# Fetching x[dst] with fp32 products, and adding x on the vector engine, in a graph layer

## The chip, the cores and the metric

The kernel runs on one core of one Trainium2 chip. Its time is the device time of one execution in microseconds (us), as the median of several runs. One core has five engines with a queue of instructions each: TensorE (PE in the profile; its weight loads are listed apart as PEld), VectorE (DVE), ScalarE (ACT), GpSimd (POOL) and SyncE (SP, which only issues transfers here). An engine works through its queue in order; engines wait for each other by semaphores.

## The reference

```python
x_i = x[dst]                                    # x: 100000 x 48, 25000 edges
x_j = x[src]
tmp = jnp.concatenate([x_i, x_j, edge_attr], axis=1)      # 25000 x 128
h = jax.nn.relu(tmp @ W1 + b1)                  # 128 hidden
msg = h @ W2 + b2
out = jax.ops.segment_sum(msg, dst, num_segments=N_NODES)
x = _layernorm(x + out, axis=-1)                # over 48 columns
```

All is fp32, and `dst` is sorted.

## The kernel before

Since `dst` is sorted, the nodes are walked in blocks of 384 (128 partitions by J = 3 nodes), and the edges of a block lie one after another, at most 128 of them (for other inputs there is a general path, which does not run). Three blocks make a "super", called g in the code; there are 88 supers, the last two short. For each super the kernel does this:

- SP loads the edge rows (`load_edges`), the nodes' rows of x (`load_nodes`, into `xs`) and stores the result (`store`). POOL gathers x[src] row by row (`gather_xsrc`, three gathers per super) and does the last scaling of the norm (`scale`).
- DVE makes a one-hot matrix of each block, edges by 384 nodes (`make_onehot`). PE turns it (`turn_onehots`, `turn_last_onehot`, line 779), ACT copies it to SBUF (`onehot_t`, line 899).
- PE fetches x[dst] as a product of the turned one-hot with the rows of x (`fetch_xdst`, line 839). To be exact with bf16 products, DVE splits `xs` into three bf16 parts: the upper half of the fp32 word, the upper half of what is left (`x_rest`), and the rest of that (`x_low`). So there are 3 blocks x 3 node columns x 3 parts = 27 products of 48 columns.
- ACT places the result in `cat` (`place_xdst`, line 921), PE turns `cat` (`turn_cat`, line 773), ACT copies that (`copy_cat`, line 887), and PE forms the hidden layer (`hidden`, line 827; ACT's `relu`, line 915) and the messages (`messages`, lines 851 and 858).
- ACT copies the messages (`copy_msg`, line 894), DVE splits them in three (`less_high_msg`, line 1040, `less_middle_msg`, line 1047), and PE adds them to the nodes with 27 products with the one-hots (`sums`, line 819). x itself was put in the same PSUM bank ahead of that by three products of the parts of x with an identity (`add_nodes`, line 805), which stand between the products of the messages.
- The norm: DVE sums over the columns (`total_sum`, line 1024), subtracts the mean (`centre`, line 1033), ACT squares (`square`, line 926), DVE sums the squares (`total_squares`, line 1082), ACT takes the root (line 931), DVE inverts (line 1090), POOL scales (line 740).

What sets the order is `walk`: each engine has a list of (lag, stage), and step t of an engine runs each stage of its list, in the order written, for super t - lag. The first 16 steps are written out, then a loop of eight steps runs, then the rest is written out. Buffers have eight places (BODY) or two (SMALL). PE's list and ACT's, which the change leaves as they are:

```python
walk(pe, ((2, turn_cat), (0, turn_onehots), (5, sums), (2, hidden), (0, turn_last_onehot), (1, fetch_xdst),
          (3, messages)))
walk(act, ((7, root), (2, copy_cat), (4, copy_msg), (0, copy_onehots), (6, square), (0, copy_last_onehot), (2, relu),
           (1, place_xdst)))
```

So ACT's `square` of super t - 6 stands ahead of `place_xdst` of super t - 1, and PE's `turn_cat` of that super is the first stage of PE's next step.

Of the kernel before, what the change touches and what calls it, by code (L numbers as in the profile page):

```python
# [5 lines left out]
P = 128  # L6
# [4 lines left out]
ALU = mybir.AluOpType  # L11
# [363 lines left out]
def gnn_resnorm_kernel(nc, x, src, dst, edge_attr, W1, b1, W2, b2, out):  # L375
# [52 lines left out]
    with ExitStack() as ctx:  # L428
# [60 lines left out]
        onehot = sb("onehot", [P, BODY, SUPER, BLOCK], BF16)  # L489
        onehot_t = sb("onehot_t", [P, SMALL, SUPER, J * P], BF16)  # L490
        cat_t = sb("cat_t", [P, SMALL, SUPER * P])
# [4 lines left out]
        xs = sb("xs", [P, BODY, SD])  # L496
        x_rest = sb("x_rest", [P, BODY, SD])
        x_low = sb("x_low", [P, BODY, SD], BF16)
        ys = sb("ys", [P, BODY, SD])
# [50 lines left out]
        msg_split = sem("msg_split")  # L550
        x_rest_ready = sem("x_rest_ready")
        x_split = sem("x_split")
        dst_counted = sem("dst_counted")
# [97 lines left out]
        def _(sp):  # L651
# [41 lines left out]
            def load_nodes(g, r, v):  # L693
                if after(g, BODY):
                    sp.wait_ge(sum_done, g - BODY + 1)
                sp.dma_start(sbuf_rows(xs, g, v), dram_rows(x, g)).then_inc(x_in[v], 16)
# [53 lines left out]
        def _(pe):  # L750
# [47 lines left out]

            def add_nodes(g, v, i):

                n, blocks, jj = shape_of(g)
                part = (upper_half(flat_of(xs, g, v)), upper_half(flat_of(x_rest, g, v)), flat_of(x_low, g, v))[i]
                if i == 0 and after(g, SMALL):
                    pe.wait_ge(centred, g - SMALL + 1)
                pe.matmul(sum_ps[v % SMALL][0:n, 0:blocks * jj * D], ident_b[0:n, 0:n], part, start=(i == 0), stop=False)  # L805

            def sums(g, r, v):

                n, blocks, jj = shape_of(g)
                ps, t, m = sum_ps[v % SMALL], v % SMALL, slice(0, blocks * D)  # L810
                msg_parts = upper_half(msg[:, t, m]), upper_half(msg_rest[:, t, m]), msg_low[:, t, m]
                pe.wait_ge(msg_split, g + 1)
                if isinstance(g, int) and g == NS - 1:
                    for i in range(PARTS):
                        add_nodes(g, v, i)
                for k in range(blocks):
                    for j in range(jj):
                        for i, part in enumerate(msg_parts):
                            last = pe.matmul(ps[0:n, (k * jj + j) * D:(k * jj + j + 1) * D], onehot[:, v, k, j * n:(j + 1) * n],  # L819
                                             part[:, k * D:(k + 1) * D], start=False,  # L820
                                             stop=(k == blocks - 1 and j == jj - 1 and i == PARTS - 1))
                last.then_inc(sum_done, 1)
# [7 lines left out]
            def fetch_xdst(g, r, v):  # L830

                n, blocks, jj = shape_of(g)
                parts = upper_half(flat_of(xs, g, v)), upper_half(flat_of(x_rest, g, v)), flat_of(x_low, g, v)
                pe.wait_ge(x_split, g + 1)
                pe.wait_ge(onehot_t_ready, first_block(g) + blocks)
                for k in range(blocks):
                    for j in range(jj):
                        for i, part in enumerate(parts):
                            last = pe.matmul(xdst_ps[:, k * D:(k + 1) * D], onehot_t[0:n, v % SMALL, k, j * P:(j + 1) * P],  # L839
                                             part[:, (k * jj + j) * D:(k * jj + j + 1) * D],  # L840
                                             start=(j == 0 and i == 0), stop=(j == jj - 1 and i == PARTS - 1))
                last.then_inc(xdst_done, 1)

            def messages(g, r, v):
                n, blocks, jj = shape_of(g)
                pe.wait_ge(hid_t_ready, g + 1)
                if after(g, 1):
                    pe.wait_ge(msg_ready, g)


                pe.matmul(msg_ps[:, 0:blocks * D], ones_b[:, :], b2_parts[:, 0:blocks, :].rearrange("p b d -> p (b d)"),  # L851
                          start=True, stop=False)
                for k in range(SUPER):
                    if after(g, 1):
                        add_nodes(g - 1, (v - 1) % BODY, k)
                    if k >= blocks:
                        continue
                    last = pe.matmul(msg_ps[:, k * D:(k + 1) * D], hid_t[:, v % SMALL, k * P:(k + 1) * P], w2[:, :],  # L858
                                     start=False, stop=(k == blocks - 1))
                    if k == blocks - 1:  # L860
                        last.then_inc(msg_done, 1)

# [79 lines left out]
        def _(dve):  # L942
# [74 lines left out]
            def sums_of(g, t):  # L1017
                n, blocks, jj = shape_of(g)
                return sum_ps[t][0:n, 0:blocks * jj * D].rearrange("p (m d) -> p m d", d=D)

            def total_sum(g, r, v):
                n, blocks, jj = shape_of(g)
                dve.wait_ge(sum_done, g + 1)
                dve.tensor_reduce(total[0:n, v % SMALL, 0:blocks * jj], sums_of(g, v % SMALL), AX_X, ALU.add).then_inc(totalled, 1)  # L1024

            def centre(g, r, v):

                n, blocks, jj = shape_of(g)
                t, m = v % SMALL, blocks * jj
                dve.wait_ge(totalled, g + 1)  # L1030
                if after(g, BODY):
                    dve.wait_ge(y_out[v], 16 * r)
                dve.scalar_tensor_tensor(out=by_node(ys, g, v), in0=total[0:n, t, 0:m].unsqueeze(2).broadcast_to([n, m, D]),
                                         scalar=-1.0 / D, in1=sums_of(g, t), op0=ALU.mult, op1=ALU.add).then_inc(centred, 1)

# [31 lines left out]

            def less_high_x(g, r, v):
                dve.wait_ge(x_in[v], 16 * (r + 1))
                dve.tensor_tensor(flat_of(x_rest, g, v), flat_of(xs, g, v), upper_half(flat_of(xs, g, v)),  # L1070
                                  ALU.subtract).then_inc(x_rest_ready, 1)

            def less_middle_x(g, r, v):
                dve.wait_ge(x_rest_ready, g + 1)
                dve.tensor_tensor(flat_of(x_low, g, v), flat_of(x_rest, g, v), upper_half(flat_of(x_rest, g, v)),
                                  ALU.subtract).then_inc(x_split, 1)

            def total_squares(g, r, v):
# [5 lines left out]
            def invert(g, r, v):  # L1084
# [3 lines left out]
                if after(g, SMALL):  # L1088
                    dve.wait_ge(normed, g - SMALL + 1)
                dve.reciprocal(rstd[0:n, t, 0:m], std[0:n, t, 0:m]).then_inc(rstd_ready, 1)  # L1090

            walk(dve, ((6, total_sum), (-1, place_dst), (-1, less_high_x), (6, centre), (-1, less_middle_x),
                       (4, less_high_msg), (-1, make_onehot), (7, invert), (4, less_middle_msg), (6, total_squares)))
            dve.wait_ge(general_done, 1)
# [26 lines left out]
```

## Time and profile before

| | us |
|---|---|
| median of 3 timed runs | 494.03 |
| lowest, highest | 492.64, 494.47 |
| span of the profiled execution | 593.7 |
| PE busy | 430.8 |
| DVE busy | 383.0 |
| POOL busy | 351.2 |
| ACT busy | 292.1 |

The profiled execution is 99.7 us longer than the median of the timed runs. The rows that the text rests on are all from that execution. A row of the timeline gives the start from the beginning of the span and how long the instruction took from its start to its end; since an engine begins the next instruction ahead of the end of the last, what an instruction costs its engine is read from start to start. "x3" means that three instructions were merged in a row. In brackets stands how long the engine was idle before it and what ended that.

### The profile page before, as it was taken

To read this page: it belongs to the slowest core of one execution; us is meant where nothing else is said; L and a number is where in the kernel's file an instruction comes from. 1 tells how busy PE (TensorE), PEld (TensorE's weight loads), DVE (VectorE), ACT (ScalarE), POOL (GpSimd) and SP (SyncE) were. 2 spreads that over 40 slices of the span, in tenths; PEclk is the share of its full clock that TensorE was granted. 3 is DMA by queue.
4 is the path that set the end of the run, shared out by engine and by line. 5 is a ranking of instruction groups with operands and counts; after the bars stand their busy time and mean duration, and the time that the engine had idled before them with its cause. 6 is when DMAs were issued, how large, how long until landed. Compare 5 with 4: busy or idle time off the path is not lost.

```text
span 593.7 us, 19546 instructions
## 1 busy us (share of the span) xinstructions
PE 430.8 (73%) x6796; PEld 368.5 (62%) x6796; DVE 383.0 (65%) x1105; ACT 292.1 (49%) x795; POOL 351.2 (59%) x365
## 2 busy tenths in 40 slices
PE   1013378797888878788788878787888878887891
PEld 1012367676767767676667767675776767766690
DVE  5423148676766678676667666776667756877673
ACT  2212147464555556464555545464555545554662
POOL 2056616767665666666665666666666666757522
PEclk9999999988988899898989888989889989999996
DMA  7833313444433434344444344343443434444422
GB/s 181 286 64 67 68 25 82 86 110 87 110 84 81 108 84 108 83 108 82 100 89 94 94 83 108 81 109 82 88 100 83 108 83 107 86 108 85 105 64 73
DMA packets 118243, 56.92 MB, mean 96 GB/s; under 512 B 46019, under 2 KB 117185, under 8 KB 118205
## 3 DMA queue, kind: packets, MB, share of 16 engines
q1 hardware_dynamic: 109440, 48.35, 32.2%
q0 software_dynamic: 8448, 6.50, 8.6%
q10 hardware_dynamic: 318, 1.61, 1.0%
q8 instruction: 20, 0.33, 0.2%
q14 instruction: 17, 0.14, 0.1%
HBM read 33.80 MB, written 22.61 MB: 95 GB/s over the span
## 4 chain that ended last, share of the span: by engine, by line
PE 66%; issue 18%; another core or an unknown queue 6%; ACT 4%; DVE 3%; DMA 1%; ACTq 0%; POOL 0%; SPq 0%; POOLq 0%; DVEq 0%
PE bank L839 14%; PE bank L827 11%; PE bank L819 10%; PE bank L779 8%; PE bank L805 8%; PE bank L858 7%; PE bank L773 7%; ACT onehot_t L899 2%; DMA next_dst_i<-in_dst_dram 1%; PE bank L851 1%; ACT sq L926 1%; ACT hid_t L915 1%; ACT cat L921 0%; ACT msg L894 0%
## 5 line engine op out<-in xcount | busy, mean ns | idle before, releaser
L732 POOL DMA_INDIRECT cat<-in_x_dram,cat x264 | 267.9, 1015 | 201.1 <-DMA cat<-edge_table 135.7
L899 ACT ACTIVATE onehot_t<-bank 128x384 bf16<-128x384 bf16 (+1 forms) x261 | 119.3, 498 | 182.1 <-remote 129.4
L1024 DVE TENSOR_REDUCE total<-bank 128x9 f32<-128x432 f32 (+1 forms) x88 | 52.8, 599 | 87.6 <-remote 86.5
L839 PE MATMUL bank<-x_low,onehot_t 128*128 128x48 bf16 (+1 forms) x782 | 86.0, 185 | 27.4 <-issue 26.9
L839 PE MATMUL bank<-x_rest,onehot_t 128*128 128x48 bf16 (+1 forms) x782 | 85.8, 186 | 26.7 <-issue 26.6
L858 PEld LDWEIGHTS bank<-w,hid_t 128*128 128x128 f32 x522 | 101.5, 208 | 4.0 <-issue 2.8
L779 PEld LDWEIGHTS bank<-ident_b,onehot 128*128 128x128 bf16 (+1 forms) x782 | 65.2, 107 | 61.4 <-issue 48.1
L839 PE MATMUL bank<-xs,onehot_t 128*128 128x48 bf16 (+1 forms) x782 | 86.6, 186 | 22.5 <-issue 22.1
L779 PE MATMUL bank<-ident_b,onehot 128*128 128x128 bf16 (+1 forms) x782 | 80.6, 236 | 24.9 <-issue 24.9
L740 POOL TENSOR_TENSOR ys<-ys,rstd 128x432 f32<-128x432 f32 (+1 forms) x88 | 80.3, 912 | 23.6 <-DVE rstd L1090 20.5
L858 PE MATMUL bank<-w,hid_t 128*128 128x48 f32 x522 | 89.9, 255 | 2.5 <-issue 2.5
L839 PEld LDWEIGHTS bank<-x_low,onehot_t 128*128 128x128 bf16 (+1 forms) x782 | 65.4, 97 | 34.5 <-issue 33.9
L839 PEld LDWEIGHTS bank<-x_rest,onehot_t 128*128 128x128 bf16 (+1 forms) x782 | 65.8, 97 | 32.5 <-issue 31.9
L827 PE MATMUL bank<-cat_t,w 128*128 128x384 f32 (+1 forms) x176 | 83.6, 559 | 1.0 <-issue 0.7
L839 PEld LDWEIGHTS bank<-xs,onehot_t 128*128 128x128 bf16 (+1 forms) x782 | 67.2, 97 | 26.3 <-issue 25.7
L1040 DVE TENSOR_TENSOR msg_rest<-msg 128x144 f32<-128x144 f32 (+1 forms) x88 | 27.1, 308 | 75.4 <-issue 37.6
L887 ACT ACTIVATE cat_t<-bank 128x384 f32<-128x384 f32 (+1 forms) x88 | 42.9, 487 | 64.1 <-PE bank L773 54.8
L819 PE MATMUL bank<-msg,onehot 128*128 128x48 bf16 (+1 forms) x782 | 73.7, 188 | 0.5 <-issue 0.5
L1064 DVE TENSOR_SCALAR onehot<-node_of,dst_in_block 128x384 bf16<-128x384 f16 x260 | 73.8, 338 | 0.1
L819 PE MATMUL bank<-msg_rest,onehot 128*128 128x48 bf16 (+1 forms) x782 | 73.0, 187 | 0.4 <-issue 0.4
L819 PE MATMUL bank<-msg_low,onehot 128*128 128x48 bf16 (+1 forms) x782 | 72.9, 187 | 0.0
L773 PE MATMUL bank<-ident,cat 128*128 128x128 f32 x261 | 52.6, 316 | 25.9 <-ACT cat L921 18.9
(91 smaller groups left out, 910.8 us busy)
## 6 DMA issues: line engine op xcount, KB each, us to landing
xs<-in_x_dram SPq DMA_DIRECT2D x86, 216.0 KB
out_dram<-ys SPq DMA_DIRECT2D x86, 216.0 KB
cat<-edge_table SPq DMA_DIRECT2D x264, 17.0 KB
cat<-in_x_dram,cat POOLq DMA_INDIRECT x264
edge_table<-table_pm SPq DMA_DIRECT2D x4, 833.0 KB, 7.5
edge_pm<-in_edge_attr_dram ACTq DMA_DIRECT2D x2, 686.0 KB, 6.0
edge_pm<-in_edge_attr_dram SPq DMA_DIRECT2D x2, 686.0 KB, 6.0
edge_pm<-in_edge_attr_dram ACTq DMA_DIRECT2D x2, 91.9 KB, 7.3
```

What stands on the lines that cost most here:

```text
L732: pool.indirect_dma_start(cat[:, v, k, D:2 * D], None, x[:, :], bass.IndirectOffsetOnAxis(ap=cat[:, v, k, P + 1:P + 2].bitcast(I32), axis= ...
L740: pool.tensor_tensor(y, y, rstd[0:n, v % SMALL, 0:blocks * jj].unsqueeze(2).broadcast_to([n, blocks * jj, D]), ALU.mult).then_inc(normed, 1)
L773: last = pe.transpose(cat_ps[:, k * P:(k + 1) * P], cat[:, v, k, 0:P], ident[:, :])
L779: last = pe.transpose(onehot_ps[k % 2][0:n, j * P:(j + 1) * P], onehot[:, v, k, j * n:(j + 1) * n], ident_b[:, :])
L805: pe.matmul(sum_ps[v % SMALL][0:n, 0:blocks * jj * D], ident_b[0:n, 0:n], part, start=(i == 0), stop=False)
L819: last = pe.matmul(ps[0:n, (k * jj + j) * D:(k * jj + j + 1) * D], onehot[:, v, k, j * n:(j + 1) * n], part[:, k * D:(k + 1) * D], start=F ...
L827: pe.matmul(hid_ps[:, 0:blocks * P], w1[:, :], cat_t[:, v % SMALL, 0:blocks * P], start=True, stop=True).then_inc(hid_done, 1)
L839: last = pe.matmul(xdst_ps[:, k * D:(k + 1) * D], onehot_t[0:n, v % SMALL, k, j * P:(j + 1) * P], part[:, (k * jj + j) * D:(k * jj + j + 1 ...
L858: last = pe.matmul(msg_ps[:, k * D:(k + 1) * D], hid_t[:, v % SMALL, k * P:(k + 1) * P], w2[:, :], start=False, stop=(k == blocks - 1))
L899: act.activation(onehot_t[0:n, v % SMALL, k, 0:jj * P], onehot_ps[k % 2][0:n, 0:jj * P], ACT.Copy).then_inc(onehot_t_ready, 1)
L1024: dve.tensor_reduce(total[0:n, v % SMALL, 0:blocks * jj], sums_of(g, v % SMALL), AX_X, ALU.add).then_inc(totalled, 1)
L1064: last = dve.tensor_scalar(onehot[:, v, k, 0:n * jj], nodes[:, 0:n * jj], dst_in_block[:, v % SMALL, k:k + 1], None, ALU.is_equal)
```

## The change

x[dst] is fetched with the fp32 rows `xs` and an fp32 `onehot_t` by nine products instead of 27; the split of x and its two buffers go. The three identity products go too; DVE adds `xs` to the sums in PSUM and writes `ys` (`add_nodes`), and `total_sum` and `centre` work on `ys` in SBUF. DVE's list is in a new order. `load_nodes` and `sums` wait for the addition.

```diff
-        onehot_t = sb("onehot_t", [P, SMALL, SUPER, J * P], BF16)
+        onehot_t = sb("onehot_t", [P, SMALL, SUPER, J * P])
...
             def load_nodes(g, r, v):
                 if after(g, BODY):
-                    sp.wait_ge(sum_done, g - BODY + 1)
+                    sp.wait_ge(added, g - BODY + 1)
...
-            def add_nodes(g, v, i):
-
-                n, blocks, jj = shape_of(g)
-                part = (upper_half(flat_of(xs, g, v)), upper_half(flat_of(x_rest, g, v)), flat_of(x_low, g, v))[i]
-                if i == 0 and after(g, SMALL):
-                    pe.wait_ge(centred, g - SMALL + 1)
-                pe.matmul(sum_ps[v % SMALL][0:n, 0:blocks * jj * D], ident_b[0:n, 0:n], part, start=(i == 0), stop=False)
...
             def sums(g, r, v):
...
-                if isinstance(g, int) and g == NS - 1:
-                    for i in range(PARTS):
-                        add_nodes(g, v, i)
+                if after(g, SMALL):
+                    pe.wait_ge(added, g - SMALL + 1)
...
-                                             part[:, k * D:(k + 1) * D], start=False,
-                                             stop=(k == blocks - 1 and j == jj - 1 and i == PARTS - 1))
+                                             part[:, k * D:(k + 1) * D], start=(i == 0), stop=(i == PARTS - 1))
...
             def fetch_xdst(g, r, v):
...
-                parts = upper_half(flat_of(xs, g, v)), upper_half(flat_of(x_rest, g, v)), flat_of(x_low, g, v)
-                pe.wait_ge(x_split, g + 1)
+                rows = flat_of(xs, g, v)
+                pe.wait_ge(x_in[v], 16 * (r + 1))
...
-                        for i, part in enumerate(parts):
-                            last = pe.matmul(xdst_ps[:, k * D:(k + 1) * D], onehot_t[0:n, v % SMALL, k, j * P:(j + 1) * P],
-                                             part[:, (k * jj + j) * D:(k * jj + j + 1) * D],
-                                             start=(j == 0 and i == 0), stop=(j == jj - 1 and i == PARTS - 1))
+                        last = pe.matmul(xdst_ps[:, k * D:(k + 1) * D], onehot_t[0:n, v % SMALL, k, j * P:(j + 1) * P],
+                                         rows[:, (k * jj + j) * D:(k * jj + j + 1) * D],
+                                         start=(j == 0), stop=(j == jj - 1))
...
+            def add_nodes(g, r, v):
+                n, blocks, jj = shape_of(g)
+                dve.wait_ge(sum_done, g + 1)
+                if after(g, BODY):
+                    dve.wait_ge(y_out[v], 16 * r)
+                dve.tensor_tensor(by_node(ys, g, v), by_node(xs, g, v), sums_of(g, v % SMALL), ALU.add).then_inc(added, 1)
...
-            walk(dve, ((6, total_sum), (-1, place_dst), (-1, less_high_x), (6, centre), (-1, less_middle_x),
-                       (4, less_high_msg), (-1, make_onehot), (7, invert), (4, less_middle_msg), (6, total_squares)))
+            walk(dve, ((6, add_nodes), (-1, place_dst), (4, less_high_msg), (6, total_sum), (-1, make_onehot), (4, less_middle_msg),
+                       (6, centre), (7, invert), (6, total_squares)))
```

One step of DVE in the steady part of the program before. `msg` and `msg_rest` are the messages, `xs` the rows of x, `bank` the PSUM bank with the sums, `ys` the result:

```order
L1024 TENSOR_REDUCE total<-bank 128x9
L1054 TENSOR_TENSOR dst_in_block<-cat,block_start 128x3
L1070 TENSOR_TENSOR x_rest<-xs 128x432
L1033 SCALAR_TENSOR_TENSOR ys<-total,bank 128x432
L1075 TENSOR_TENSOR x_low<-x_rest 128x432
L1040 TENSOR_TENSOR msg_rest<-msg 128x144
L1064 TENSOR_SCALAR onehot<-node_of,dst_in_block 128x384 x3
L1090 RECIPROCAL rstd<-std 128x9
L1047 TENSOR_TENSOR msg_low<-msg_rest 128x144
L1082 TENSOR_REDUCE sq_total<-sq 128x9
```

The same step of DVE in the changed program:

```order
L1007 TENSOR_TENSOR ys<-xs,bank 128x432
L1041 TENSOR_TENSOR dst_in_block<-cat,block_start 128x3
L1027 TENSOR_TENSOR msg_rest<-msg 128x144
L1012 TENSOR_REDUCE total<-ys 128x9
L1051 TENSOR_SCALAR onehot<-node_of,dst_in_block 128x384 x3
L1034 TENSOR_TENSOR msg_low<-msg_rest 128x144
L1020 SCALAR_TENSOR_TENSOR ys<-total,ys 128x432
L1067 RECIPROCAL rstd<-std 128x9
L1059 TENSOR_REDUCE sq_total<-sq 128x9
```

`centre` (ys from total) stood ahead of the subtraction for `msg_rest`; it now stands behind it, behind the one-hots and behind `msg_low`, and one short instruction ahead of the sum of the squares.

PE at the end of a step before, from the last product of the fetch to the transposes that begin the next step (`w` is W2, `hid_t` the hidden layer):

```order
L839 MATMUL bank<-x_low,onehot_t 128x48
L851 MATMUL bank<-b_parts,ones_b 128x144
L805 MATMUL bank<-xs,ident_b 128x432
L858 MATMUL bank<-w,hid_t 128x48
L805 MATMUL bank<-x_rest,ident_b 128x432
L858 MATMUL bank<-w,hid_t 128x48
L805 MATMUL bank<-x_low,ident_b 128x432
L858 MATMUL bank<-w,hid_t 128x48
L773 MATMUL bank<-ident,cat 128x128 x3
```

And in the changed program, from the last transposes of the one-hots on:

```order
L776 MATMUL bank<-ident_b,onehot 128x128 x3
L825 MATMUL bank<-xs,onehot_t 128x48 x9
L837 MATMUL bank<-b_parts,ones_b 128x144
L840 MATMUL bank<-w,hid_t 128x48 x3
L770 MATMUL bank<-ident,cat 128x128 x3
```

The fetch is nine products in a row, and nothing stands between the products of the messages.

## Rows read from the trace of the kernel before

**Rows 1.** The page, busy us, share of the span and instructions of each engine:
```profile
PE 430.8 (73%) x6796; PEld 368.5 (62%) x6796; DVE 383.0 (65%) x1105; ACT 292.1 (49%) x795; POOL 351.2 (59%) x365
```

**Rows 2.** The waits: engine and line, waited for; us in total, times, longest:
```profile
PE bank L839 <- issue: 75.7, 161, 1.2
```

**Rows 3.** Busy time by stretch: stretch, length, each engine, granted clock, DMA share, GB/s:
```profile
83.47:569.50 486.03, 397.69 (x6396) 342.03 (x6395) 341.05 (x975) 265.12 (x736) 312.07 (x314) 0.93 0.42 93
```

**Rows 4.** Timeline of PE, an early step and a late one: start, us, instruction:
```profile
83.47 0.51 PE L773 MATMUL bank<-ident,cat 128*128 128x128 f32 x3
...
85.73 0.19 PE L839 MATMUL bank<-xs,onehot_t 128*128 128x48 bf16 x1
...
86.42 0.22 PE L851 MATMUL bank<-b_parts,ones_b 128*128 128x144 bf16 x1
...
86.67 0.32 PE L858 MATMUL bank<-w,hid_t 128*128 128x48 f32 x2
86.82 0.35 PE L805 MATMUL bank<-x_rest,ident_b 128*128 128x432 bf16 x1
...
87.50 0.51 PE L773 MATMUL bank<-ident,cat 128*128 128x128 f32 x3
...
569.50 0.51 PE L773 MATMUL bank<-ident,cat 128*128 128x128 f32 x3
```

**Rows 5.** Timeline of POOL, the gathers and the scaling:
```profile
92.08 0.95 POOL L732 DMA_INDIRECT cat<-in_x_dram,cat  x1 [0.30 <-issue]
93.33 0.95 POOL L732 DMA_INDIRECT cat<-in_x_dram,cat  x1 [0.30 <-issue]
94.79 0.91 POOL L740 TENSOR_TENSOR ys<-ys,rstd 128x432 f32<-128x432 f32 x1 [0.51 <-issue]
95.85 0.99 POOL L732 DMA_INDIRECT cat<-in_x_dram,cat  x1
```

**Rows 6.** Timeline of PE and of its weight loads, first steps (two windows):
```profile
65.64 0.90 PE L773 MATMUL bank<-ident,cat 128*128 128x128 f32 x3 [9.37 <-ACT cat L921]
...
70.00 0.73 PEld L858 LDWEIGHTS bank<-w,hid_t 128*128 128x128 f32 x3
...
70.00 1.37 PEld L858 LDWEIGHTS bank<-w,hid_t 128*128 128x128 f32 x6
```

**Rows 7.** Timeline of ACT, three places:
```profile
65.29 0.29 ACT L921 ACTIVATE cat<-bank 128x144 f32<-128x144 f32 x1 [9.11 <-remote]
...
84.02 0.49 ACT L887 ACTIVATE cat_t<-bank 128x384 f32<-128x384 f32 x1 [1.14 <-PE bank L773]
84.41 0.28 ACT L894 ACTIVATE msg<-bank 128x144 f32<-128x144 f32 x1
...
85.93 0.49 ACT L899 ACTIVATE onehot_t<-bank 128x384 bf16<-128x384 bf16 x1 [0.47 <-PE bank L779]
86.32 0.57 ACT L915 ACTIVATE hid_t<-bank,b1c 128x384 f32<-128x384 f32 x1
86.78 0.29 ACT L921 ACTIVATE cat<-bank 128x144 f32<-128x144 f32 x1
...
578.76 0.56 ACT L926 ACTIVATE sq<-ys 128x432 f32<-128x432 f32 x1 [0.71 <-DVE ys L1033]
```

**Rows 8.** Timeline of DVE, an early step and one at the end:
```profile
84.72 0.31 DVE L1040 TENSOR_TENSOR msg_rest<-msg 128x144 f32<-128x144 f32 x1 [2.40 <-ACT msg L894]
84.95 0.77 DVE L1064 TENSOR_SCALAR onehot<-node_of,dst_in_block 128x384 bf16<-128x384 f16 x3
85.64 0.30 DVE L1047 TENSOR_TENSOR msg_low<-msg_rest 128x144 bf16<-128x144 f32 x1
85.86 0.60 DVE L1024 TENSOR_REDUCE total<-bank 128x9 f32<-128x432 f32 x1
86.38 0.15 DVE L1054 TENSOR_TENSOR dst_in_block<-cat,block_start 128x3 f32<-128x3 f32 x1
...
578.12 0.60 DVE L1033 SCALAR_TENSOR_TENSOR ys<-total,bank 128x432 f32<-128x432 f32 x1
```

More of the change, by code:

```diff
@@ L550, in gnn_resnorm_kernel @@
         msg_split = sem("msg_split")
-        x_rest_ready = sem("x_rest_ready")
-        x_split = sem("x_split")
+        added = sem("added")
         dst_counted = sem("dst_counted")
@@ L852, in messages @@
                           start=True, stop=False)
[L853 to L857, printed above, removed]
+                for k in range(blocks):
                     last = pe.matmul(msg_ps[:, k * D:(k + 1) * D], hid_t[:, v % SMALL, k * P:(k + 1) * P], w2[:, :],
                                      start=False, stop=(k == blocks - 1))
-                    if k == blocks - 1:
-                        last.then_inc(msg_done, 1)
+                last.then_inc(msg_done, 1)
             walk(pe, ((2, turn_cat), (0, turn_onehots), (5, sums), (2, hidden), (0, turn_last_onehot), (1, fetch_xdst),
@@ L1019, in sums_of @@
                 return sum_ps[t][0:n, 0:blocks * jj * D].rearrange("p (m d) -> p m d", d=D)
+            def add_nodes(g, r, v):
[4 more added lines that the diff above has]
+                dve.tensor_tensor(by_node(ys, g, v), by_node(xs, g, v), sums_of(g, v % SMALL), ALU.add).then_inc(added, 1)
             def total_sum(g, r, v):
                 n, blocks, jj = shape_of(g)
-                dve.wait_ge(sum_done, g + 1)
-                dve.tensor_reduce(total[0:n, v % SMALL, 0:blocks * jj], sums_of(g, v % SMALL), AX_X, ALU.add).then_inc(totalled, 1)
+                dve.wait_ge(added, g + 1)
+                dve.tensor_reduce(total[0:n, v % SMALL, 0:blocks * jj], by_node(ys, g, v), AX_X, ALU.add).then_inc(totalled, 1)
             def centre(g, r, v):
@@ L1030, in centre @@
                 dve.wait_ge(totalled, g + 1)
[L1031 to L1034, printed above, removed]
+                y = by_node(ys, g, v)
+                dve.scalar_tensor_tensor(out=y, in0=total[0:n, t, 0:m].unsqueeze(2).broadcast_to([n, m, D]),
+                                         scalar=-1.0 / D, in1=y, op0=ALU.mult, op1=ALU.add).then_inc(centred, 1)
             def less_high_msg(g, r, v):
@@ L1066, in make_onehot @@
                 last.then_inc(onehot_ready, 1)
[L1068 to L1076, printed above, removed]
             def total_squares(g, r, v):
```

2 lines of the change are left out of this document (removed).

## The prediction

> **What bounds the kernel now.** I read the views in the order of the row groups. First the shares: no engine is above three quarters of the span, and PE, DVE and POOL are close to each other [rows 1], so what matters is the length of one step of each engine's loop, not the busy share. Then the waits: the largest of PE's are gaps ahead of the products of line 839 in which it waits for nothing that is shown, 75.7 us [rows 2]. Over the long middle stretch the granted clock is 0.93 on average [rows 3], that is, about 14% of the time at the lower of TensorE's two levels (1.2 GHz) and the rest at 2.4 GHz.
>
> An early step shows PE without any gap: transposes of `cat` start at 83.47 and again at 87.50 [rows 4], so PE's own work for one step (three blocks, one "super") takes **4.03 us** at the upper level. The same transposes start at 569.50 for g = 85, and 83.47 was g = 3: 82 steps in 486.0 us, 5.93 us each in the profiled run. POOL has its own minimum: gathers start 1.25 us apart (92.08, 93.33), one takes 0.95, and from the scaling to the next gather 1.06 passes (94.79, 95.85) [rows 5]: 1.25 + 1.25 + 0.95 + 1.06 = **4.51 us**.
>
> The profiled span is 593.7 us, the median of the timed runs 494.0, so profiling itself costs about 100 us. I take the 107.7 us outside the 82 steps (593.7 - 486.0) as the same in both; then a timed step is (494.0 - 107.7) / 82 = **4.71 us**. That fits POOL's 4.51 with small losses better than PE's 4.03, so the timed kernel seems to be held by POOL's queue, with PE about 0.7 us per step behind it. This split is an inference; the sum below uses only differences to 4.71.
>
> **The change on PE.** The fetch of x[dst] is 27 bf16 products in 0.69 us (85.73 to 86.42) [rows 4]. It becomes nine fp32 products. The nearest rows are the fp32 products of line 858, also 48 columns wide against 128x128 fp32 weights. Each leaves two records. In the first step, with no other product between them, three weight loads take 0.73 us and six take 1.37 [rows 6]: 0.213 us per record. That was at the lower level, for the three transposes beside them take 0.90 [rows 6] where they take 0.51 at the upper [rows 4]. Half of it is 0.107. The bounds: not below 0.075 (in the messages an fp32 product starts at 86.67 and the next identity product at 86.82 [rows 4], 0.15 us for two records, of which one has its load beside the product ahead), not above 0.213. I take 0.107 since only those rows have consecutive fp32 products: 18 records are 1.92 us, **+1.23** (bounds +0.66 and +3.1). The fp32 weights stay 128 wide, and the moving side is read as loaded, so there is nothing else.
>
> The three identity products per step go. The messages are then one bias product, 0.06, and six records: 0.70 in place of 1.08 (86.42 to 87.50 [rows 4]), **-0.38**. The 27 products of the sums stay; only their start and stop marks change. PE's own step: 4.03 + 1.23 - 0.38 = **4.88 us**.
>
> The Trainium skill, "FP8 and Floating Point Precision", section "TensorE Precision Notes", says that true FP32 takes four passes through the array. As an estimate from that, a product of 48 columns would be four times the 0.026 us of a bf16 one, 0.10 us; fetch 0.92, messages 0.37, PE's step 3.55. The trace disagrees, with 0.213 us per product at the upper level: it is the loads of weights that stand 0.213 us apart at the lower one [rows 6].
>
> **The change on DVE and ACT.** DVE loses two subtractions per step (0.52 us from start to start, like the reduction from 85.86 to 86.38 [rows 8]) and gains one addition of the same 432 columns, which I price the same; between 0.5 and 0.6. It is 0.5 us lighter. ACT writes `onehot_t` in fp32: the 384-column copy to fp32 has 0.49 us and the one to bf16 0.49 [rows 7], so nothing. SP's load of x now waits for the addition instead of the last product of the sums, half a step later; queued behind it are a store and the edge loads of two steps ahead, seven PE steps from their use, so I cost it at zero. The sums wait for the addition of two supers back, which stands one DVE step earlier; zero too. ys is written by the addition, an op earlier than by `centre`, with the store of eight supers back long done.
>
> What counts is the new order on DVE. Before, `centre`(g-6) stood ahead of the subtraction `less_high_msg`(g-4), so ACT's square had its input early. Now it stands behind `less_high_msg`, which waits for ACT's copy of the messages in the same step, and behind the total, the three one-hots and `less_middle_msg`. ACT's queue is strict: square waits for `centre`, and behind it stand the last one-hot copy, the relu and `place_xdst`, for which PE's next transposes wait. This closes a loop through all three engines within one step. From start to start, in us:
>
> PE's transposes to ACT's copy of cat 0.55 (83.47, 84.02); to the copy of msg 0.39 (84.41); to DVE's msg_rest 0.31 (84.72); to the next on DVE 0.23 (84.95); the total 0.52 (85.86 to 86.38); three one-hots 0.69 (84.95 to 85.64); msg_low 0.22 (to 85.86); `centre` to square 0.64 (578.12, 578.76); square to the next on ACT 0.46 (as relu, 86.32 to 86.78, of nearly the same length); the last one-hot copy 0.39 (85.93 to 86.32); relu 0.46; `place_xdst` to PE's transposes 0.35 (65.29, 65.64) [rows 4, 6 to 8].
>
> The sum is 0.55 + 0.39 + 0.31 + 0.23 + 0.52 + 0.69 + 0.22 + 0.64 + 0.46 + 0.39 + 0.46 + 0.35 = **5.21 us**. It is longer than PE's 4.88 and POOL's 4.51, and no queue can run ahead in it, as every member waits for one of the same step. PE's end of the fetch (transposes, sums, hidden layer, then 1.92 us: about 4.4 us after the step's start) comes before ACT reaches `place_xdst` at 4.86, so the fetch's own price hardly matters.
>
> **The forecast.** A step of 5.21 us holds at the upper clock. Where the clock is at 1.2 GHz, PE's 4.88 becomes 9.76 and holds the step. With 14% of the time there, the mean is 1 / (0.86/5.21 + 0.14/9.76) = 5.57. Without the slack of 0.7 us that PE has today nothing absorbs such stretches, but the timed run may have fewer of them; I take the middle, 5.39. Then 494.0 + 82 x (5.39 - 4.71) = 550, and some 2 us for the first fetch at the lower clock (18 x 0.213 = 3.8 against twice 0.69): **552 us**. Its own range goes from 5.21 (494 + 41 + 2 = 537) to 5.57 (567).
>
> **Rivals.** (1) The loop has slack that I don't see, and PE alone decides: 82 x (4.88 - 4.71) = +14, with the first fetch 510 us. For it: all handoffs are single rows. Against: the waits in the code leave no second route. (2) The clock. PE now waits 0.3 us in every step, its work in between has changed, and the trace shows that the granted clock is not held at the upper level throughout [rows 3]; if the lower level held 30% of the time, the step were 6.06 and the time 605. Against: 5.93 us per step in the profile left PE waiting more than that, and the clock was at the lower level only 14% of the time. (3) The other side, faster: profiling stretches the rows. The profiled run is 1.20 times the timed one; if each handoff is shorter by that too, the loop is 5.21 / 1.20 = 4.34 and no bound, and what makes 4.71 today are gaps in PE's supply of instructions at line 839, 4.71 - 4.03 = 0.68 per step. With 18 records for 27 products they shrink to 0.45; PE's step is 4.88 / 1.20 + 0.45 = 4.52, that is 494 - 16 = 478. It decides once the handoffs are under 0.90 of their rows (5.21 x 0.90 = 4.69). Against: semaphore waits of 0.04 us in the rows have no room for it. (4) No change: neither the loop nor the products cost, PE stays below POOL's 4.51, and the time stays near 494. By the four-pass rule of the Trainium skill ("FP8 and Floating Point Precision") PE's step would be 3.55 and the second half of this rival true; the trace bears out neither half.
>
> **Chances.** The loop 0.64, PE alone 0.12, the clock 0.11, faster 0.08, no change 0.05. The likeliest is 552. The range takes in PE alone and a mild case of the clock: 505 to 582. About 0.5%, 2.5 us, is what a measurement of this kernel can tell from no change. Slower by more: 0.64 + 0.12 + 0.11 = 0.87; within: 0.05; faster: 0.08.
>
> **What would show it.** Right: PE's transposes start some 5.2 us apart at the fewest; ACT's square waits for `centre` in nearly every step, DVE's squares reduction for the square, PE's transposes for `place_xdst`; fp32 fetch records 0.107 us apart. Wrong: square finds its input ready, PE runs without a gap of its own at 4.9, or the fetch records stand much closer. The forecast falls if the timed kernel is not at the step that I derived, above all if POOL or the gaps behave otherwise without the profiler.

## The result, and the profile after

The changed kernel takes **534.0 us** (median of 4 runs, 532.3 to 535.4), the kernel before 494.3 (median of 4). The ratio is 1.082, with a 95% interval from 1.078 to 1.086: clearly slower. (A ratio, here and below, counts only the runs within 1.5% of the fastest run of the same kernel.) The profiled execution has a span of 530.3 us, close to the timed runs, unlike that of the kernel before (593.7).

The page of the changed kernel, to be read against [rows 1]: busy time by engine, the granted clock in 40 slices, and the first groups of instructions (busy and mean ns, then the idle time before them and what ended it):

```profile
PE 461.9 (87%) x5750; PEld 415.8 (78%) x5750; DVE 397.2 (75%) x1017; ACT 292.5 (55%) x795; POOL 348.9 (66%) x365
...
PEclk9999998999998989999999999999999999999985
...
L825 PE MATMUL bank<-xs,onehot_t 128*128 128x48 f32 x1564 | 189.8, 276 | 0.0
L825 PEld LDWEIGHTS bank<-xs,onehot_t 128*128 128x128 f32 x1564 | 184.0, 194 | 0.6
L907 ACT ACTIVATE sq<-ys 128x432 f32<-128x432 f32 (+1 forms) x88 | 49.1, 558 | 143.1 <-DVE ys L1020 141.6
...
L1041 DVE TENSOR_TENSOR dst_in_block<-cat,block_start 128x3 f32<-128x3 f32 (+1 forms) x88 | 76.2, 866 | 22.9 <-DMA cat<-edge_table 22.9
```

Two rows stand out. ACT waits 141.6 us for `centre` ahead of its square, 87 times of 88. And an instruction on three columns, `place_dst` (line 1041), takes 866 ns on average, against 150 in [rows 8]. The gaps of [rows 2] ahead of the fetch are gone.

The waits (engine and line, waited for; us in total, times, longest) name the members of the loop that the prediction drew:

```profile
ACT sq L907 <- DVE ys L1020: 141.6, 87, 2.8
...
DVE sq_total L1059 <- ACT sq L907: 44.2, 88, 0.6
DVE msg_rest L1027 <- ACT msg L875: 43.7, 51, 3.6
ACT cat_t L868 <- PE bank L770: 41.8, 86, 1.0
...
PEld bank L770 <- ACT cat L902: 19.7, 64, 1.4
```

And the timeline of one step of it (start, us, instruction), the rows that answer to [rows 4, 7, 8]:

```profile
304.50 0.54 PE L770 MATMUL bank<-ident,cat 128*128 128x128 f32 x3 [0.21 <-ACT cat L902]
...
305.08 0.49 ACT L868 ACTIVATE cat_t<-bank 128x384 f32<-128x384 f32 x1 [0.53 <-PE bank L770]
...
305.47 0.28 ACT L875 ACTIVATE msg<-bank 128x144 f32<-128x144 f32 x1
...
305.79 0.31 DVE L1027 TENSOR_TENSOR msg_rest<-msg 128x144 f32<-128x144 f32 x1
...
306.01 0.60 DVE L1012 TENSOR_REDUCE total<-ys 128x9 f32<-128x432 f32 x1
...
306.53 0.91 DVE L1051 TENSOR_SCALAR onehot<-node_of,dst_in_block 128x384 bf16<-128x384 f16 x3
...
307.36 0.30 DVE L1034 TENSOR_TENSOR msg_low<-msg_rest 128x144 bf16<-128x144 f32 x1
...
307.57 0.60 DVE L1020 SCALAR_TENSOR_TENSOR ys<-total,ys 128x432 f32<-128x432 f32 x1
...
308.20 0.56 ACT L907 ACTIVATE sq<-ys 128x432 f32<-128x432 f32 x1 [1.68 <-DVE ys L1020]
308.67 0.47 ACT L880 ACTIVATE onehot_t<-bank 128x384 f32<-128x384 bf16 x1
...
309.05 0.57 ACT L896 ACTIVATE hid_t<-bank,b1c 128x384 f32<-128x384 f32 x1
...
309.51 0.29 ACT L902 ACTIVATE cat<-bank 128x144 f32<-128x144 f32 x1
...
309.85 0.55 PE L770 MATMUL bank<-ident,cat 128*128 128x128 f32 x3 [0.18 <-ACT cat L902]
```

From 304.50 to 309.85 are 5.35 us, one step. The reader can add it up: 0.58, 0.39, 0.32, 0.22, 0.52, 0.83, 0.21, 0.63, 0.47, 0.38, 0.46, 0.34. Eleven of the twelve terms are within 0.03 us of the prediction's; the three one-hots took 0.83 us instead of 0.69.

### The profile page after: what moved, and what is told of

It is laid out like the page before. It is cut to its first block, busy times and chain, and to the rows that moved or that the text cites. A ratio compares the mean times of both kernels' runs of the same rounds, so it can differ in the third digit from the quotient of the medians.

```text
span 530.3 us, 17427 instructions
## 1 busy us (share of the span) xinstructions
PE 461.9 (87%) x5750; PEld 415.8 (78%) x5750; DVE 397.2 (75%) x1017; ACT 292.5 (55%) x795; POOL 348.9 (66%) x365
## 4 chain that ended last, share of the span: by engine, by line
DVE 41%; PE 19%; ACT 17%; issue 14%; DMA 3%; SPq 3%; DVEq 1%; ACTq 1%; POOL 0%; POOLq 0%
DVE onehot L1051 9%; DVE total L1012 9%; DVE ys L1020 8%; DVE dst_in_block L1041 7%; PE bank L825 6%; PE bank L770 6%; ACT sq L907 5%; DVE ys L1007 4%; ACT onehot_t L880 3%; ACT hid_t L896 3%; DVE msg_low L1034 3%; PE bank L814 2%; ACT msg L875 2%; ACT cat L902 2%; PE bank L807 2%
## 5 line engine op out<-in xcount | busy, mean ns | idle before, releaser
L825 PE MATMUL bank<-xs,onehot_t 128*128 128x48 f32 x1564 | 189.8, 276 | 0.0
L825 PEld LDWEIGHTS bank<-xs,onehot_t 128*128 128x128 f32 x1564 | 184.0, 194 | 0.6
L907 ACT ACTIVATE sq<-ys 128x432 f32<-128x432 f32 (+1 forms) x88 | 49.1, 558 | 143.1 <-DVE ys L1020 141.6
L880 ACT ACTIVATE onehot_t<-bank 128x384 f32<-128x384 bf16 (+1 forms) x261 | 117.6, 492 | 17.7 <-PE bank L776 17.7
L1041 DVE TENSOR_TENSOR dst_in_block<-cat,block_start 128x3 f32<-128x3 f32 (+1 forms) x88 | 76.2, 866 | 22.9 <-DMA cat<-edge_table 22.9
L1059 DVE TENSOR_REDUCE sq_total<-sq 128x9 f32<-128x432 f32 (+1 forms) x88 | 52.6, 598 | 44.2 <-ACT sq L907 44.2
L814 PE MATMUL bank<-cat_t,w 128*128 128x384 f32 (+1 forms) x176 | 80.5, 540 | 0.9 <-ACT cat_t L868 0.9
L840 PE MATMUL bank<-w,hid_t 128*128 128x48 f32 x522 | 71.0, 272 | 0.0
L1027 DVE TENSOR_TENSOR msg_rest<-msg 128x144 f32<-128x144 f32 (+1 forms) x88 | 30.1, 342 | 48.7 <-ACT msg L875 43.7
L807 PEld LDWEIGHTS bank<-msg,onehot 128*128 128x128 bf16 (+1 forms) x782 | 63.9, 97 | 3.4 <-DVE msg_low L1034 3.4
L840 PEld LDWEIGHTS bank<-w,hid_t 128*128 128x128 f32 x522 | 65.2, 192 | 0.0
L807 PEld LDWEIGHTS bank<-msg_rest,onehot 128*128 128x128 bf16 (+1 forms) x782 | 62.5, 97 | 0.0
```

The costliest lines, as they stand in the source:

```text
L814: pe.matmul(hid_ps[:, 0:blocks * P], w1[:, :], cat_t[:, v % SMALL, 0:blocks * P], start=True, stop=True).then_inc(hid_done, 1)
L880: act.activation(onehot_t[0:n, v % SMALL, k, 0:jj * P], onehot_ps[k % 2][0:n, 0:jj * P], ACT.Copy).then_inc(onehot_t_ready, 1)
L907: act.activation(flat_of(sq, g, v % SMALL), flat_of(ys, g, v), ACT.Square).then_inc(squared, 1)
L1041: dve.tensor_tensor(dst_in_block[:, v % SMALL, 0:blocks], cat[:, v, 0:blocks, P], block_start[:, bass.ds(first_block(g), blocks)], ALU.sub ...
```

## Experiments

Times are medians. The step is the mean distance of PE's transposes of `cat` from g = 3 to g = 85 in the profiled execution, over 82, and "outside" is the rest of the span.

| kernel | us | ratio to before (95%) | step | outside |
|---|---|---|---|---|
| changed | 534.0 | 1.082 (1.078 to 1.086) | 5.39 | 88.3 |
| early_centre | 501.2 | 1.011 (1.006 to 1.016) | 4.97 | 92.4 |
| before_late_centre | 520.6 | 1.055 (1.051 to 1.060) | 5.26 | 88.0 |
| fp32_fetch | 535.3 | 1.085 (1.080 to 1.090) | 5.34 | 96.0 |
| dve_add | 508.2 | 1.031 (1.026 to 1.036) | 5.13 | 85.0 |
| before_again | 493.1 (one run) | | 4.98 | 82.8 |
| before_two_gathers | 483.4 | 0.995 (0.989 to 1.000) | 4.85 | 83.4 |
| before_no_identity | 492.1 | 1.012 (1.001 to 1.023) | 4.98 | 81.1 |
| before_dve_scale | 476.9 | 0.981 (0.967 to 0.995) | 4.83 | 79.4 |
| dve_scale_ahead | 476.1 | 0.966 (0.962 to 0.971) | 4.81 | 78.6 |
| after_dve_scale | 528.4 | 1.089 (1.072 to 1.107) | 5.35 | 85.0 |
| early_dve_scale | 496.2 | 1.005 (1.002 to 1.009) | 4.97 | 88.5 |

Four ratios have to be read with care: those of before_two_gathers, before_no_identity, before_dve_scale and after_dve_scale. They were measured together, beside 13 runs of the kernel before, and only two of these count, the lowest, at 484.6 and 488.6 us. The other eleven took 492.0 to 497.0, close to the kernel before beside the other kernels (490.8 to 495.5). Against the median of all 13, 493.3 us, the quotients are 0.980, 0.998, 0.967 and 1.071, and all four ratios given for them are above these by more than 0.01. None of the four counts as a measured difference on its ratio alone; below they are read by their times and steps.

### The order of DVE alone, taken away and put in

My theory was the loop through ACT's square. The rival was that the fp32 products alone cost the time on PE. The first kernel takes the order out of the changed kernel:

```diff
-            walk(dve, ((6, add_nodes), (-1, place_dst), (4, less_high_msg), (6, total_sum), (-1, make_onehot), (4, less_middle_msg),
-                       (6, centre), (7, invert), (6, total_squares)))
+            walk(dve, ((6, add_nodes), (-1, place_dst), (6, total_sum), (6, centre), (4, less_high_msg), (-1, make_onehot),
+                       (7, invert), (4, less_middle_msg), (6, total_squares)))
```

> The changed kernel with one edit: in DVE's list the total and the centring stand ahead of the split of the messages again, so ACT's square finds its input early. Nothing is left out. If the loop through ACT's square (5.21 us a step) and DVE's own chain behind it set the 534 us, the step falls to PE's own 4.9 to 5.0 us and the time to 494 to 503. If instead the price of the fp32 products on PE sets it, nothing changes: 530 to 536. In the profile ACT's waits for ys, 141.6 us in the changed kernel, should be under 30.

Measured: 501.2 us, within the 494 to 503 expected (ten runs, 494.9 to 502.7). Of the 40 us that the change costs, 33 go with this one line, and what is left is no difference beyond 2% to the kernel before. 80 of the 82 steps are 4.97 us, and in the middle of the profile PE does not pause; busy time by stretch (PE, PEld, DVE, ACT, POOL, granted clock, DMA share, GB/s):

```profile
83.00:460.00 377.00, 377.00 (x5013) 349.29 (x5012) 340.35 (x833) 253.12 (x684) 299.17 (x303) 1.00 0.47 115
```

The wait for `ys` ahead of the square, 141.6 us in the changed kernel, is 4.9 us in five waits here. What PE waited for before, it now has in time; PE's own work is the limit.

The second kernel puts the order into the kernel before, with bf16 products and identity products:

```diff
-            walk(dve, ((6, total_sum), (-1, place_dst), (-1, less_high_x), (6, centre), (-1, less_middle_x),
-                       (4, less_high_msg), (-1, make_onehot), (7, invert), (4, less_middle_msg), (6, total_squares)))
+            walk(dve, ((-1, less_high_x), (-1, place_dst), (-1, less_middle_x), (4, less_high_msg), (6, total_sum),
+                       (-1, make_onehot), (4, less_middle_msg), (6, centre), (7, invert), (6, total_squares)))
```

> The kernel before with one edit: DVE's list in the order of the changed kernel (the centring behind the split of the messages, the total and the one-hots). bf16 products and identity products as before, nothing left out. If the order makes the loop, this kernel is slow as well, 5.2 to 5.4 us a step, 520 to 540 us. If the slowdown comes from the fp32 products it stays at 490 to 497.

Measured: 520.6 us, as expected of the loop, and most steps are 5.21 to 5.30 us, 53 of the 82 at 5.21 or 5.22. Its waits show the same first member, and PE now also waits for `centre` ahead of the identity products, as these need the bank that it reads:

```profile
ACT sq L926 <- DVE ys L1033: 135.7, 87, 2.4
...
PE bank L805 <- DVE ys L1033: 38.0, 83, 1.2
```

So the order alone costs 27 us, with no fp32 product in the fetch. The loop is shown from both sides. PE's wait ahead of the identity products is a second consequence of the late `centre`, and this run doesn't separate its price; the changed kernel has the loop without it.

### The two parts of the change apart

```diff
-        onehot_t = sb("onehot_t", [P, SMALL, SUPER, J * P], BF16)
+        onehot_t = sb("onehot_t", [P, SMALL, SUPER, J * P])
...
             def add_nodes(g, v, i):
...
+                if i == 0:
+                    pe.wait_ge(x_split, g + 1)
...
-                        for i, part in enumerate(parts):
-                            last = pe.matmul(xdst_ps[:, k * D:(k + 1) * D], onehot_t[0:n, v % SMALL, k, j * P:(j + 1) * P],
-                                             part[:, (k * jj + j) * D:(k * jj + j + 1) * D],
-                                             start=(j == 0 and i == 0), stop=(j == jj - 1 and i == PARTS - 1))
+                        last = pe.matmul(xdst_ps[:, k * D:(k + 1) * D], onehot_t[0:n, v % SMALL, k, j * P:(j + 1) * P],
+                                         rows[:, (k * jj + j) * D:(k * jj + j + 1) * D],
+                                         start=(j == 0), stop=(j == jj - 1))
```

> The kernel before with the nine fp32 products for the fetch alone; x is still split and added by PE with identity products, DVE's order is that of before. By the sum PE's own step is 4.03 + 1.23 = 5.26 us, which then holds: with a step of 4.95 in the timed kernel before (494.0 less the 88.4 us outside the steps in the profile of after, over 82), 494 + 82 x 0.31 = 519 us (512 to 528). If a product costs only 0.15 us, PE needs 4.7 and the time stays at 490 to 497.

Measured: 535.3 us, above the range given. PE's timeline in this kernel:

```profile
303.00 2.16 PE L840 MATMUL bank<-xs,onehot_t 128*128 128x48 f32 x18
305.00 0.23 PE L852 MATMUL bank<-b_parts,ones_b 128*128 128x144 bf16 x1
```

The fetch takes 2.00 us from start to start, 0.111 per record, where I had put 1.92 and 0.107. Against the 0.69 of the bf16 fetch that is +1.31, and 4.03 + 1.31 = 5.34 is the step, within 0.02 us in all but two of the 82. The step was off by 0.08; the rest of the miss is outside the steps: 96.0 us where I had put 88.4.

The other part, with the centring early, is the fetch and the split of x as before, and x added by DVE:

```diff
-            walk(dve, ((6, add_nodes), (-1, place_dst), (4, less_high_msg), (6, total_sum), (-1, make_onehot), (4, less_middle_msg),
-                       (6, centre), (7, invert), (6, total_squares)))
+            walk(dve, ((6, add_nodes), (-1, less_high_x), (6, total_sum), (-1, place_dst), (6, centre), (-1, less_middle_x),
+                       (4, less_high_msg), (-1, make_onehot), (7, invert), (4, less_middle_msg), (6, total_squares)))
```

(The diff is against the changed kernel; the fetch is that of before.)

> The other part alone: the fetch with 27 bf16 products and the split of x as before, but x added by DVE and no identity products; the centring stands early. PE's own step falls to 4.03 - 0.38 = 3.65 us, DVE's grows to about 4.5. If POOL (4.51) or DVE holds the kernel before, the time stays at 488 to 500. If PE with its gaps holds it, 0.38 x 82 = 31 us go: 460 to 468.

Measured: 508.2 us, slower than before and outside both expectations. PE had lost work, and the kernel became slower: it is not PE that holds it. DVE is busy 92% of the span, and one instruction that I priced at 0.6 us takes twice that:

```profile
L1062 DVE TENSOR_TENSOR x_rest<-xs 128x432 f32<-128x432 f32 (+1 forms) x88 | 106.9, 1215 | 24.8 <-DMA xs<-in_x_dram 24.8
L1056 DVE TENSOR_SCALAR onehot<-node_of,dst_in_block 128x384 bf16<-128x384 f16 x260 | 69.0, 322 | 0.0
L1025 DVE SCALAR_TENSOR_TENSOR ys<-total,ys 128x432 f32<-128x432 f32 (+1 forms) x88 | 53.0, 602 | 0.2
```

### What holds the kernel before

This and the 100 us between the profile and the timed runs made me doubt the trace on which the prediction rests. The unchanged kernel was profiled again:

> The kernel before, unchanged, profiled once more. Every other kernel here had a profiled span within 6 us of its timed runs; that of the kernel before was 100 us over, with gaps of 0.3 to 0.5 us ahead of the products of the fetch. If that belongs to the kernel, the span is near 594 again. If it was one disturbed execution, the span is near 491, the mean step 4.9 to 5.0 us, PE has no such gaps, and DVE is busy 90% with instructions of two SBUF operands lengthened by up to 0.9 us at POOL's scaling.

Measured: a span of 491.0 us. The profile shown ahead of the prediction was one disturbed execution, and what disturbed it is not known; the gaps ahead of the fetch do not belong to the kernel. The new one shows who holds it:

```profile
PE 386.8 (79%) x6796; PEld 325.4 (66%) x6796; DVE 444.4 (91%) x1105; ACT 290.7 (59%) x795; POOL 369.4 (75%) x365
```

and by stretch:

```profile
300.00:310.00 10.00, 8.68 (x158) 7.27 (x156) 10.00 (x25) 6.35 (x19) 8.42 (x9) 1.00 0.51 114
```

DVE is busy without a pause, and from 100 to 440 us it is busy 337.4 of 340. The timeline of DVE and POOL in the same place shows with what:

```profile
300.51 1.96 DVE L1064 TENSOR_SCALAR onehot<-node_of,dst_in_block 128x384 bf16<-128x384 f16 x3
301.43 0.92 POOL L740 TENSOR_TENSOR ys<-ys,rstd 128x432 f32<-128x432 f32 x1
302.40 0.20 DVE L1090 RECIPROCAL rstd<-std 128x9 f32<-128x9 f32 x1
```

The three one-hots, 0.77 us in [rows 8], take 1.96 where POOL's scaling runs beside them (it ends at 302.35, they at 302.47). In the same way early_centre has its long instruction at `centre`, at 303.60 for 1.49 us beside the scaling from 303.69:

```profile
303.60 1.49 DVE L1020 SCALAR_TENSOR_TENSOR ys<-total,ys 128x432 f32<-128x432 f32 x1
303.69 0.93 POOL L737 TENSOR_TENSOR ys<-ys,rstd 128x432 f32<-128x432 f32 x1
```

dve_add has it at `x_rest` and the changed kernel at `place_dst`. Those that wait read two tensors from SBUF, or are the one-hots with their 16-bit operands. The sum of the squares, which reads one, and the addition from PSUM are not lengthened in these profiles.

A lengthened instruction ends at a fixed distance behind the end of the scaling, whenever it began: a one-hot 0.13 us behind it, `place_dst` 0.03, `x_low` 0.48. So the one that is caught loses more than the 0.92 us of the scaling: `place_dst` took up to 1.54 us in the changed kernel, for 0.15 alone. In most steps of the new profile (the two one-hot groups start 5.04 us apart) the one-hots take 1.89 us from start to start in place of 0.69; that is 3.84 us of DVE's own work and 1.20 of waiting. From 100 to 440 us each of the 68 scalings lengthens one DVE instruction, by 1.18 us on average; in the disturbed profile only 7 of 55 did.

The Trainium skill has this mechanism: in "SBUF — State Buffer", section "SBUF: two separate sides", VectorE and GpSimd share a pair of ports under an exclusive lock, taken by a VectorE instruction with two SBUF operands or in a 2-port perf mode and by a GpSimd one; whichever starts first has it for its whole instruction, and the other waits. The traces here agree on who waits and until when, with 0.6 us grown to 1.5. On who is first they do not agree as recorded: in the changed kernel `place_dst` started up to 0.59 us ahead of the recorded start of the scaling and waited all the same. Whether POOL holds the ports from ahead of its recorded start is not shown.

Three runs test it from three sides. POOL's own load first (one gather of three left out, from the ninth super on, and PE waits for one fewer):

```diff
-                for k in range(SUPER):
+                for k in range(SUPER if isinstance(r, int) and r == 0 else SUPER - 1):
                     pool.indirect_dma_start(
```

> The kernel before, but from the ninth super on POOL gathers x[src] only for two of the three blocks (the third keeps old rows, so its messages are left wrong). POOL's own step falls from 4.51 to 3.26 us. If POOL's queue holds the kernel before, the time falls by at least 82 x 0.4 = 33 us, to 460 or less. If DVE with its wait for POOL's scaling holds it, the time stays at 485 to 497.

Measured: 483.4 us, 10 us under the median of the kernel before and just below the 485 to 497 expected. POOL's minimum of 4.51 us fell to 3.26 and the step only from 4.98 to 4.85. POOL's queue does not hold it. The trace shows where the 0.13 us come from: DVE is still busy (339.4 of 340 us from 100 to 440), but the scaling now meets mostly `place_dst`, and what it adds to a step of DVE fell from 1.18 to 1.06 us. PE's load next (x is left out of the sums):

```diff
-                    if after(g, 1):
-                        add_nodes(g - 1, (v - 1) % BODY, k)
```

> The kernel before without the three identity products per step, so x is not added to the sums (left out of the result); the products of the sums carry start marks of their own. PE's own step falls from 4.03 to 3.65 us, nothing else changes. If PE holds the kernel before, 20 to 31 us go (462 to 474). If DVE or POOL holds it, 488 to 497.

Measured: 492.1 us, no gain, as expected if PE isn't the limit. The step is 4.98 us as before, and so is what the scaling adds to it, 1.18. PE does not hold it. In dve_add the same sum comes out: there the scaling adds 0.74 us to a step of 5.13, which leaves 4.39, about DVE's own 3.84 and the one instruction of 0.52 that it has more. Last, the scaling is taken off POOL, so that nothing is there to wait for, at the price of one more instruction on DVE:

```diff
-            walk(pool, ((1 - AHEAD, gather_xsrc), (8, scale)))
+            walk(pool, ((1 - AHEAD, gather_xsrc),))
...
-                       (4, less_high_msg), (-1, make_onehot), (7, invert), (4, less_middle_msg), (6, total_squares)))
+                       (4, less_high_msg), (-1, make_onehot), (7, invert), (4, less_middle_msg), (7, scale), (6, total_squares)))
```

> The kernel before with the last scaling of the norm moved from POOL to DVE (behind msg_low); nothing left out. Theory: the kernel before is held by DVE, 4.02 us of work plus the wait of a DVE instruction with two operands in SBUF for POOL's scaling (up to 0.9 us): 4.92 us a step. Then DVE needs 4.02 + 0.52 = 4.54, and the time falls by 82 x 0.38 = 31 to about 463 us (458 to 475). If POOL's queue held it at 4.51 plus losses, POOL now needs 3.75 and DVE 4.54: about the same. The rival in which DVE's work is additive and no wait exists: 4.92 + 0.52, slower, 530 us.

Measured: 476.9 us, 16 under the median of the kernel before, all four runs below its lowest. DVE, which was busy without a pause, got one more instruction, and the kernel is faster. POOL is lighter too, but before_two_gathers, with POOL lighter still, had 0.13 us a step in all. What went are the waits for the scaling; the lengths are back at those of the instructions alone:

```profile
L1056 DVE TENSOR_SCALAR onehot<-node_of,dst_in_block 128x384 bf16<-128x384 f16 x260 | 68.0, 319 | 0.0
L1062 DVE TENSOR_TENSOR x_rest<-xs 128x432 f32<-128x432 f32 (+1 forms) x88 | 53.1, 603 | 47.2 <-DMA xs<-in_x_dram 46.2 <-issue 0.2
```

It gained half of what I expected; the step is 4.83, not 4.54, and DVE is no longer the only limit, busy 307.4 us of the 340. Among its longest waits are those for transfers, so the last variant issues them a step earlier:

```diff
-AHEAD = 3
-X_AHEAD = 2
+AHEAD = 4
+X_AHEAD = 3
```

> The kernel before with the scaling on DVE and, in addition, the edge rows and the rows of x loaded one step earlier (AHEAD 4 and X_AHEAD 3 in place of 3 and 2). Nothing left out. The profile of the run with the scaling on DVE shows 46 us of DVE waiting for x and 117 us of POOL waiting for edge rows, at a mean step of 4.83 us where DVE's work is 4.54. If those waits are on the path, up to 82 x 0.29 = 24 us go (453 to 470). If not, 475 to 479.

Measured: 476.1 us, the same as without the earlier loads. The waits for transfers were not what was missing; what holds these two kernels at 4.8 us stays open. They are the fastest of the study, the second 3.4% under the kernel before by a ratio that counts all 13 of its runs.

### The changed kernel without the scaling on POOL

The same move of `scale` in the changed kernel, with DVE's list otherwise as it is there:

```diff
-                       (6, centre), (7, invert), (6, total_squares)))
+                       (6, centre), (7, invert), (7, scale), (6, total_squares)))
```

> The changed kernel with the last scaling moved from POOL to DVE, behind the inversion, in front of the sum of the squares, where DVE waits for ACT's square anyway; nothing left out. Theory: the loop through the square alone is 5.21 us and the rest up to the mean of 5.39 comes from DVE waiting for POOL's scaling in front of the split of the messages. Then the steps are 5.21 to 5.24 throughout and the time is 534 - 82 x 0.16 = 521 us (518 to 525). If the scaling is simply one more DVE instruction on the chain: 534 or more.

Measured: 528.4 us, 6 less than the changed kernel and between the two expectations (its four runs go from 525.6 to 533.4). Its profile has the square waiting as before, and no long `place_dst`:

```profile
ACT sq L899 <- DVE ys L1012: 139.8, 88, 1.8
DVE msg_rest L1019 <- ACT msg L867: 104.8, 85, 3.9
```

DVE now waits 104.8 us for the messages, 43.7 before: it arrives early and the loop holds it all the same. Most steps are 5.21 to 5.45, so the expectation of 5.21 to 5.24 throughout was wrong. The mean went from 5.39 to 5.35: in the changed kernel three steps were long because `less_high_msg` itself was caught by the scaling (1.50 us instead of 0.31, at 114.57 us), and here there is none of them. The long `place_dst` cost next to nothing there. From 85 to 480 us `less_high_msg`, behind it, began within 0.04 us of the end of ACT's copy of the messages in 69 of 73 cases, so DVE would have waited anyway. DVE's wait for the scaling is a small part in the changed kernel.

And in early_centre:

```diff
-                       (7, invert), (4, less_middle_msg), (6, total_squares)))
+                       (7, invert), (4, less_middle_msg), (7, scale), (6, total_squares)))
```

> The changed kernel with both orders mended: the centring early (as in the run early_centre) and the last scaling on DVE. Nothing left out. Theory: early_centre was held by PE alone, at 4.97 us in every step, and DVE's waits for POOL's scaling, which its profile shows, lay beside PE's work. So the time stays at 501 us (496 to 504). The rival, that those waits cost time here too, gives 475 to 485.

Measured: 496.2 us, at the lower end of the 496 to 504 expected (ten runs, 492.7 to 500.6). Its steps are those of early_centre, 80 of 82 at 4.97 us, so PE holds both; the 5 us less lie outside the steps (88.5 against 92.4) or in the spread.

## Why the prediction was right, and where it was not

The forecast was 552 us, slower; measured were 534. The way and the mechanism were right; the size was 18 us too much.

- **The loop.** Right, and right to the hundredth where nothing else comes in: 22 of the 82 steps of the changed kernel are 5.18 to 5.24 us and only the first and the last two are shorter, and with the order alone 53 are 5.21 or 5.22. Taking it away gave 33 us back, putting it into the kernel before cost 27.
- **The mean step.** 5.39 was forecast and 5.39 measured, by luck. I had lengthened 5.21 by stretches at 1.2 GHz, 14% of the time. The granted clock from 83.5 to 500 us is 0.99 on average, that is 2% of the time. Seven steps of the 82 are 5.91 to 6.55 us: three overlap the stretches in which the clock was at 0.50 (80.5, 159.0 and 186.3 us), in three more `less_high_msg` waited for the scaling, and one has a table load of 1.28 us on ACT. The other 75 have a mean of 5.30, and what lengthens those are the one-hots (the row for the 0.69 was from a stretch in which POOL did nothing, which I did not look at). Of 24 such steps in which the three take under 0.72 us from start to start, 20 are 5.18 to 5.23 us; the 21 in which they take over 0.83 are all 5.33 to 5.50.
- **The step of the timed kernel before, 4.71 us.** This is the step that failed. It rested on the 107.7 us outside the steps of a disturbed profile being the same in the timed runs. The undisturbed one has 82.8, and the step is 4.98. With that, 82 x (5.39 - 4.98) = 34 us, and the 5.5 us more outside the steps (88.3 against 82.8), make 39 of the 40 measured. The sum of the prediction had 56 in place of 34. A profile 100 us over the timed runs should have been read as a warning on its stalls, not only as an offset.
- **What holds the kernel before.** Wrong. I named POOL's queue, as its 4.51 us lay nearest to 4.71. It is DVE, with 3.8 us of its own and 1.2 of waiting for POOL's scaling. The disturbed trace had hidden the waits: there only 7 of 55 scalings from 100 to 440 us met a DVE instruction that had to wait, here all 68.
- **PE's price.** Nearly right: +1.31 for the fetch (+1.23 forecast), PE's own step 4.97 (4.88). With two loads of 128 fp32 columns for each product, nine products take three times as long as 27 in bf16. The prediction's estimate from four passes, taken alone, would have given 0.92 us for the fetch; it took 2.00.
- **The edits costed at nothing** held up as far as the waits show: neither the load of x nor the sums nor the copy to fp32 (492 ns against 498 before) is among the long waits.
- **The rivals.** PE alone, priced at 510, was the case of early_centre at 501. Faster and no change fell with the loop, and the clock with the 0.99 above.

That fp32_fetch and the changed kernel have the same time is a coincidence of two limits: PE at 5.34 us a step in the one, the loop at 5.21 to 5.5 in the other.

## What to carry to other kernels

When an instruction is moved in one engine's queue, follow what the next engine's queue has behind the instruction that waits for it: a loop from start to start through three queues can be added up from single rows, and here it gave the step to the hundredth. Fewer products are not less work where each has an fp32 weight load. And before any sum is made on a profile that is much longer than the timed runs, profile again: its idle time can hide the true limit.

## What the runs showed of the hardware

DVE instructions with two operands in SBUF, and the 16-bit one-hots, waited for POOL's TENSOR_TENSOR of 0.92 us until it ended, also where they had started up to 0.59 us ahead of its recorded start: a three-column subtraction took up to 1.54 us in the changed kernel, 0.15 otherwise. Moving that work from POOL to DVE made the kernel faster (493.3 to 476.9 us, and a ratio of 0.966 with the loads a step earlier) though DVE was already the limit. An fp32 product with 128 weight columns and 48 moving ones costs 0.222 us at 2.4 GHz when others of its kind stand before it, against 0.026 in bf16. POOL's gathers lengthen DVE's one-hots too. In all 13 profiles, from 85 to 460 us, a one-hot with neither a gather nor the scaling beside it took at most 0.32 us (227 of them), and each of the 265 over 0.35 us that had no scaling beside it, up to 0.55, had a gather. Most one-hots beside a gather take 0.31 all the same, so what in a gather does it is not shown.
